# Second attention of a four-layer block: two batches prepared ahead, norms and the copy of K on ScalarE, one Newton chain for two norms

## The reference

```python
x = x + attn_a(layernorm(x), W_attn, b_attn, W_proj, b_proj)   # 16 heads, rotary, causal
x = x + ffn(layernorm(x), expert_sel, keys, values)            # 64 experts, each token to its best 4
x = x + attn_b(layernorm(x), WQ, WK, WV)                       # one head, local band, see below
x = x + ffn(layernorm(x), expert_sel, keys, values)            # the same experts again

def attn_b(inputs, WQ, WK, WV):
    q, k, v = (einsum('bth,hd->btd', inputs, W) for W in (WQ, WK, WV))
    score = einsum('bqd,bkd->bqk', q, k) / sqrt(128)
    score = score * band          # band is 1 within 32 below and 31 above, else 0
    return einsum('bqk,bkd->bqd', softmax(score), v)   # scores outside the band are 0, not -inf

def ffn(x, expert_sel, keys, values):
    sel_val, sel_idx = top_k(sigmoid(xf @ expert_sel.T), 4)
    # sum over the chosen experts of (relu(xf @ keys[e]) * gate) @ values[e]
```

## Time and profile before

| | us |
|---|---|
| median of three runs | 1124.91 |
| lowest and highest | 1121.94, 1127.12 |
| the profiled execution | 1120.72 |
| its span, first to last instruction | 1119.0 |
| mean granted clock of TensorE, as a share of 2.4 GHz | 0.86 |

### The profile page before, as it was taken

How to read it: one execution, slowest core, us unless ns; L and a number is a source line. 1 busy time by engine, 2 the same in 40 slices (tenths; PEclk the granted TensorE clock), 3 DMA queues, 4 the chain that set the end, 5 groups by cost and what they waited for, 6 DMA issues and landing times.

```text
span 1119.0 us, 22668 instructions
## 1 busy us (share of the span) xinstructions
PE 802.9 (72%) x7290; PEld 590.3 (53%) x7290; DVE 752.1 (67%) x2101; ACT 559.8 (50%) x1505; POOL 729.7 (65%) x860
## 2 busy tenths in 40 slices
PE   2799988787878877679789986566478776994000
PEld 0444444444434432669789875445468776993000
DVE  3687898988878842576566788898676773773111
ACT  1167766776747665456546544444436553662000
POOL 6344648898975758665676457777745246666776
PEclk9889999999969988889989996785689898997555
DMA  6455655543237223359868642111156566995222
GB/s 191 135 200 203 210 163 175 189 142 117 67 91 237 61 70 100 107 162 273 240 172 239 180 127 69 48 51 51 49 150 172 147 181 180 263 283 164 71 61 63
DMA packets 206548, 163.82 MB, mean 146 GB/s; under 512 B 15968, under 2 KB 191072, under 8 KB 206432
## 3 DMA queue, kind: packets, MB, share of 16 engines
q1 hardware_dynamic: 183968, 110.43, 34.5%
q0 software_dynamic: 16384, 33.59, 10.4%
q10 hardware_dynamic: 6080, 18.35, 4.4%
HBM read 78.94 MB, written 83.36 MB: 145 GB/s over the span
## 4 chain that ended last, share of the span: by engine, by line
PE 34%; DVE 19%; POOL 19%; issue 12%; DMA 10%; ACT 5%; ACTq 0%; POOLq 0%; DVEq 0%; SPq 0%
PE ps L786 5%; PE ps L687 5%; POOL sorted_rows L1742 4%; PE ps L795 4%; DMA v_aug<-result_rows,dest 3%; PE ps L646 3%; PE ps L775 3%; DMA x_scaled<-result_rows,dest 3%; POOL y_heads L1756 2%; ACT arena L993 2%; POOL arena L1788 2%; POOL x_scaled L1756 2%; DVE row_max L1226 2%; POOL xn L1763 1%; PE ps L734 1%
## 5 line engine op out<-in xcount | busy, mean ns | idle before, releaser
L993 ACT ACTIVATE arena<-ps 128x512 f32<-128x512 f32 x320 | 183.0, 598 | 74.9 <-PE ps L619 73.7
L1742 POOL DMA_INDIRECT sorted_rows<-v_aug,dest x144 | 143.5, 997 | 97.9 <-issue 33.4
L1425 DVE COPY arena<-ps 128x512 f32<-128x512 f32 x128 | 88.1, 689 | 98.7 <-PE ps L775 98.3
L786 PE MATMUL ps<-arena 128*128 128x128 f32 x1024 | 145.6, 288 | 10.4 <-DVE arena L1425 9.1
L646 PE MATMUL ps<-arena 64*128 64x128 bf16 (+3 forms) x576 | 129.9, 305 | 28.8 <-DMA arena<-k_parts 15.2
L1226 DVE TENSOR_REDUCE row_max<-ps 128x1 f32<-128x512 f32 (+1 forms) x192 | 126.8, 681 | 30.6 <-PE ps L666 29.6
L982 ACT COPY arena<-ps 128x512 f32<-128x512 f32 x128 | 74.9, 586 | 144.6 <-PE ps L795 142.3
L786 PEld LDWEIGHTS ps<-arena 128*128 128x128 f32 x1024 | 133.3, 203 | 13.8 <-DVE arena L1425 10.0
L795 PE MATMUL ps<-arena 128*128 x1024 | 138.7, 279 | 0.9 <-ACT arena L982 0.9
L1742 POOL DMA_INDIRECT sorted_rows<-x_scaled,dest x112 | 111.7, 997 | 36.2 <-issue 23.7
L619 PE MATMUL ps<-arena 64*128 64x512 bf16 (+3 forms) x512 | 124.4, 311 | 15.0 <-ACT arena L993 12.4
(11 more groups left out here) (219 smaller groups left out, 1683.4 us busy)
## 6 DMA issues: line engine op xcount, KB each, us to landing
arena<-sorted_rows SPq DMA_DIRECT2D x128, 256.0 KB, 3.9
result_rows<-arena SPq DMA_DIRECT2D x128, 256.0 KB, 2.8
sorted_rows<-arena ACTq DMA_DIRECT2D x16, 1024.0 KB, 5.1
arena<-q_parts SPq DMA_DIRECT2D x16, 512.0 KB, 3.9
arena<-k_parts SPq DMA_DIRECT2D x16, 512.0 KB, 5.0
q_parts<-parts SPq DMA_DIRECT2D x52, 128.0 KB, 2.8
k_parts<-parts SPq DMA_DIRECT2D x38, 128.0 KB, 2.9
sorted_rows<-v_aug,dest POOLq DMA_INDIRECT x144
```

Of the source, the lines that this page charges most:

```text
L786: mm = pe.matmul(ps[:, e_bank(2, layer, half, n), P * i:P * i + P], ktile[:, v, P * i:P * i + P], xtt[:, v, P * i:P * i + P], start=True, ...
L993: nc.scalar.activation(prob[:, grp % 2, pr % 2, PROB_AT[u]:PROB_AT[u] + T], ps[:, v % 2, :], ACT.Exp, scale=SCALE_A).then_inc(exp_done, 1)
L1742: g.indirect_dma_start(sorted_d[b // HALF][:, :], bass.IndirectOffsetOnAxis(dest[:, 16 * b + n:16 * b + n + 1], 0), scaled_rows(layer, b)[ ...
```

## The change

Iteration b now prepares batch b + 2 instead of b + 1, so the loop starts at b = -2 and has one iteration more. The router's norm of batch b is applied in iteration b itself instead of b + 1, so NT and LG move there; choice, ranks, positions, scaling and scatter stay one iteration later. DVE takes the statistics of batch b and of batch b + 2 one after the other and runs one Newton chain on both (`inverse_roots`), which ends in a new small operation, minus mean times inverse root. ACT applies both norms with it as bias and the root as scale (N3 for the router, N2 for the attention: four activations each) and copies K. The four additions of a batch's gathered rows stand at one place of DVE's iteration instead of four. The orders of PE, ACT and DVE, the banks, and the places of the expert steps change with it: (0, 1) has 15, 14 and 5 steps beside iterations -2, -1 and 0; (1, 0) has 8 and 14 beside iterations 7 and 8 and the remaining 12 behind them. POOL's order of transfers and SP's order do not change.

```diff
@@ -87,15 +87,14 @@
 
 
 
-BJOBS = [(1, "S01", 0), (3, "S23", 0), (5, "NT", -1), (6, "LG", -1), (7, "P01", 0), (1, "P23", 0), (3, "XT", 1), (5, "O", 0),
-         (6, "Q", 1), (7, "K", 1), (1, "RK", -1), (3, "V", 1), (5, "VO", 1), (6, "TB", -1)]
-LAST_IT_B = B + 1
+BJOBS = [(1, "S01", 0), (3, "S23", 0), (7, "P01", 0), (1, "P23", 0), (5, "O", 0), (1, "RK", -1), (5, "NT", 0), (3, "XT", 2),
+         (6, "LG", 0), (6, "Q", 2), (7, "K", 2), (3, "V", 2), (5, "VO", 1), (6, "TB", -1)]
+FIRST_IT_B, LAST_IT_B = -2, B + 1
 WIN = 192
 OUTSIDE = T - WIN
 PLACES = 14
-BESIDE = {(0, 1): {-1: (3, 0, 0, 1, 1, 0) + 8 * (1,), 0: PLACES * (1,), 1: 7 * (1, 0)},
-          (1, 0): {6: (0, 0, 0, 0, 0, 0, 1, 1, 1, 1, 1, 1, 1, 0), 7: (1, 0, 1, 1, 0, 1, 1, 1, 1, 0, 1, 0, 1, 0),
-                   8: (1, 1, 1, 1, 1, 1, 0, 1, 0, 1, 1, 1, 0, 1)}}
+BESIDE = {(0, 1): {-2: (3, 1, 1, 0) + 10 * (1,), -1: PLACES * (1,), 0: (1, 0, 1, 0, 1, 0, 1, 0, 1, 0, 0, 0, 0, 0)},
+          (1, 0): {7: 6 * (0,) + 8 * (1,), 8: PLACES * (1,)}}
 
 
...
@@ -896,26 +900,26 @@
                         attention_b(name, b)
 
             apart(0, expert_step)
-            for it in range(-1, LAST_IT_B + 1):
+            for it in range(FIRST_IT_B, LAST_IT_B + 1):
                 attend(it, "S01", "S23")
                 beside(it, 0)
                 beside(it, 1)
+                attend(it, "P01")
+                beside(it, 2)
+                attend(it, "P23")
+                beside(it, 3)
+                attend(it, "O")
+                beside(it, 4)
+                attend(it, "RK")
+                beside(it, 5)
+                beside(it, 6)
                 attend(it, "NT")
-                beside(it, 2)
-                attend(it, "LG", "P01")
-                beside(it, 3)
-                attend(it, "P23")
-                beside(it, 4)
-                attend(it, "O")
-                beside(it, 5)
-                attend(it, "XT")
-                beside(it, 6)
+                beside(it, 7)
+                attend(it, "XT", "LG")
+                beside(it, 8)
...
@@ -1080,7 +1084,22 @@
                 act.wait_ge(bank_ready[bank], n + 1)
                 return ps[:, bank, :], bank_free[bank]
 
+            def apply_norm(i, b, dst, done):
+
+                for t in range(TT):
+                    nc.scalar.activation(dst[:, t, :], x[:, TT * b + t, :], ACT.Identity, bias=negb[:, i, t:t + 1],
+                                         scale=rsb[:, i, t:t + 1]).then_inc(done, 1)
+
             def attention_b(name, b):
+                if name == "N3":
+                    act.wait_ge(shifts, b + 3)
+                    act.wait_ge(scaled, 16 * (B + b - 1))
+                    apply_norm(1, b, xn1[:, b % 2], norm3)
+                    return
+                if name == "N2":
+                    act.wait_ge(shifts, b + 1)
+                    apply_norm(0, b, xn0, norm2)
+                    return
                 if name == "E":
                     act.wait_ge(nrow_done, b + 1)
                     nc.scalar.activation(probw[:, b % 2, :, WIN], nrow[:, b % 2, :], ACT.Exp)
@@ -1099,6 +1118,8 @@
                     nc.scalar.copy(ntt[:, :], o).then_inc(free, 1)
                 elif name == "Q":
                     nc.scalar.copy(qt[b % 2], o).then_inc(free, 1)
+                elif name == "K":
+                    nc.scalar.copy(kt[b % 2], o).then_inc(free, 1)
                 elif name == "V":
                     nc.scalar.copy(va[b % 2], o)
...
@@ -1128,29 +1149,28 @@
 
             apart(0, expert_step)
             act.wait_ge(band_made, BANDS)
-            for it in range(-1, LAST_IT_B + 1):
+            for it in range(FIRST_IT_B, LAST_IT_B + 1):
                 attend(it, "E")
                 beside(it, 0)
                 beside(it, 1)
-                attend(it, "NT")
+                attend(it, "P01")
                 beside(it, 2)
-                attend(it, "LG", "P01")
-                beside(it, 3)
                 attend(it, "P23")
-                beside(it, 4)
-                beside(it, 5)
-                attend(it, "XT")
-                beside(it, 6)
-                attend(it, "Q")
+                for place in (3, 4, 5, 6):
+                    beside(it, place)
+                attend(it, "N3", "N2", "NT")
                 beside(it, 7)
+                attend(it, "XT", "LG")
+                beside(it, 8)
+                attend(it, "Q", "K")
+                beside(it, 9)
                 attend(it, "V")
-                for place in (8, 9, 10):
-                    beside(it, place)
+                beside(it, 10)
...
-                for t in range(TT):
-                    nc.vector.tensor_scalar(dst[:, t, :], src[:, t, :], mv[:, t, 0:1], rs[:, t:t + 1],
-                                            ALU.subtract, ALU.mult).then_inc(seq, 1)
-                    if t % 2:
-                        yield 0.7
-
             roots = count()
 
-            def inverse_root(rs, b, seq, rstd):
-
-                q = 3 * ROOT_STEPS * next(roots)
-                dve.wait_ge(seq, 13 * b + 9)
-                nc.vector.tensor_scalar(guess[:, :].bitcast(I32), rs[:, :].bitcast(I32), -0.5, ROOT_BITS,
-                                        ALU.mult, ALU.add).then_inc(root_seq, 1)
+            def inverse_roots(lo, hi):
+
+                n = next(roots)
+                q = 3 * ROOT_STEPS * n
+                rs, y, half = rsb[:, lo:hi, :], guess[:, lo:hi, :], slope[:, lo:hi, :]
+                nc.vector.tensor_scalar(y.bitcast(I32), rs.bitcast(I32), -0.5, ROOT_BITS, ALU.mult, ALU.add).then_inc(root_seq, 1)
                 for i in range(ROOT_STEPS):
                     dve.wait_ge(root_seq, q + 3 * i + 1)
-                    nc.vector.scalar_tensor_tensor(out=slope[:, :], in0=rs[:, :], scalar=-0.5, in1=guess[:, :],
-                                                   op0=ALU.mult, op1=ALU.mult).then_inc(root_seq, 1)
+                    nc.vector.scalar_tensor_tensor(out=half, in0=rs, scalar=-0.5, in1=y, op0=ALU.mult, op1=ALU.mult).then_inc(root_seq, 1)
                     dve.wait_ge(root_seq, q + 3 * i + 2)
-                    nc.vector.tensor_tensor(slope[:, :], slope[:, :], guess[:, :], ALU.mult).then_inc(root_seq, 1)
+                    nc.vector.tensor_tensor(half, half, y, ALU.mult).then_inc(root_seq, 1)
                     dve.wait_ge(root_seq, q + 3 * i + 3)
                     last = i == ROOT_STEPS - 1
-                    nc.vector.scalar_tensor_tensor(out=(rs if last else guess)[:, :], in0=slope[:, :], scalar=1.5, in1=guess[:, :],
-                                                   op0=ALU.add, op1=ALU.mult).then_inc(rstd if last else root_seq, 1)
+                    nc.vector.scalar_tensor_tensor(out=rs if last else y, in0=half, scalar=1.5, in1=y,
+                                                   op0=ALU.add, op1=ALU.mult).then_inc(rstd_b if last else root_seq, 1)
+                dve.wait_ge(rstd_b, n + 1)
...
@@ -1578,10 +1586,8 @@
                                                          op0=ALU.mult, op1=ALU.add)
                 res.then_inc(free, 1)
                 dve.wait_ge(*evacuated("O", b))
-                if b:
-                    dve.wait_ge(ln3, 13 * b)
-                finish(ln_stats(x[:, TT * b:TT * b + TT, :], st1, mv1, rs1, b, ln3))
-                inverse_root(rs1, b, ln3, rstd3)
+                finish(ln_stats(x[:, TT * b:TT * b + TT, :], st1, mvb[:, 1], rsb[:, 1, :], b, ln3, norm3))
+                dve.wait_ge(ln3, 9 * b + 9)
 
...
@@ -1612,69 +1618,54 @@
 
             apart(0, expert_step)
             dve.wait_ge(band_made, BANDS)
-            for c in range(TOPK):
-                add_rows(0, 0, c)
-
-            for b in range(-1, LAST_IT_B + 1):
-                r, nxt = b - 1, b + 1
-                attend, route, prepare = 0 <= b < B, 0 <= r < B, nxt < B
+
+            for b in range(FIRST_IT_B, LAST_IT_B + 1):
+                r, far = b - 1, b + 2
+                attend, route, prepare = 0 <= b < B, 0 <= r < B, far < B
                 if attend:
                     score_rows(b)
-                beside(b, 0)
-                if route:
-                    dve.wait_ge(scaled, 16 * (B + r - 1))
-                    finish(ln_apply(x[:, TT * r:TT * r + TT, :], mv1, rs1, xn1[:, r % 2], r, ln3, rstd3))
-                beside(b, 1)
-                beside(b, 2)
-                beside(b, 3)
-                if prepare:
-                    combined_stats(nxt)
-                beside(b, 4)
-                if prepare:
-                    if nxt:
-                        bank, n = bjob["XT", b]
-                        dve.wait_ge(bank_ready[bank], n + 1)
-                    finish(ln_apply(x[:, TT * nxt:TT * nxt + TT, :], mv0, rs0, xn0, nxt, ln2, rstd2))
-                add_soon(b + 2, 0)
-                beside(b, 5)
+                for place in (0, 1, 2):
+                    beside(b, place)
                 if route:
```

(65 more changed lines are left out.)

30 lines of the change are left out of this document (10 added, 20 removed).

## The result

| | before | after |
|---|---|---|
| median of four runs, us | 1124.95 | 1148.21 |
| lowest and highest | 1121.94, 1127.12 | 1144.40, 1151.77 |
| the profiled execution, and its span | 1120.72, 1119.0 | 1151.77, 1150.0 |
| granted clock, mean | 0.860 | 0.845 |

After takes 1.0208 times as long, 95% interval 1.0161 to 1.0255. Of the 31.0, 3.7 arise ahead of the second attention: the first product of the experts (0, 1) starts at 557.85 us before and at 561.54 after. That is how executions differ and no cost of the change: in the twelve kernels of the experiments, which are the same as after up to there, it starts between 557.2 and 561.2 us.

A forecast was written before the change was run, and what follows sets the result against it. DVE bounded iterations, POOL second; afterwards ACT's queue would close the loop at 31.7 us. Batch 7's Newton end 870.7 plus 57.5 gave 928.2, gathers 949.0, plus 180.8 and 2.3 a 1132.1 us span; forecast 1138, range 1108 to 1149.

The forecast's parts named there:

- The period: Second attention's loop, one Newton chain end to the next: 31.7 us through ACT's queue, bounds 25.8 and 33.5.
- one hole: DVE's timeline in iterations 2 to 5: idle for 6 us or more ahead of the output product.
- R(1): R(b) is the end of the Newton chain of batch b's router norm; R(1) was forecast at 688.5 us.
- E: ACT's exponentials of the next batch: to start directly behind the sixteenth scaling, without waiting for DVE, 17.4 us into the period.
- The activation: ACT's eight norm activations with scale and bias: 0.30 us each, taken from the scaling's row, upper bound 0.44.
- the first rival: Second attention's loop: DVE still closes it, faster; at a 25.8 us period 1104 us on the median; chance 0.21.
- The 4.6 us that the prediction took off DVE: DVE's work per iteration: norm applications, K's copy and a Newton chain removed, one small operation added; 4.6 of 25.0 us.
- The head: First iterations of the second attention, beside layer 0's expert steps: batch 0's Newton chain ends at 660.6 us, batch 1's 688.5.
- R(7) to the last batch's scatter: From the end of batch 7's Newton chain to the last scatter's start: 57.5 us, against 47.3 before.
- no step ran ahead of R(7): Layer 1, half 0: no expert step ahead of batch 7's Newton chain end; first expert product after 860 us.
- The rest: From the last scatter's start to the end of the span: 201.5 us as before, plus 2.3 for slower gathers.
- the last rival: Slower than forecast: lower clock throughout, activations at 0.40 us, five periods 9 us longer, 1147 us; chance 0.12.

The follow-up runs named there:

- e1: The kernel after, with ACT's sixteen scalings moved from directly ahead of the next iteration's exponentials to later in that iteration: 1130.0 us, ratio to before 1.0063.
- e4: The kernel after, with DVE taking the statistics of batch b+2 ahead of the output of batch b instead of behind it: 1138.5 us, ratio to before 1.0136.
- e6: The kernel after, with 36 and 44 unread identity transposes added in PE's two idle stretches of iterations 1 to 6: 1133.2 us, ratio to before 1.0106.
- e7: The kernel after, its work reordered: next batch's scores, exponentials and transposes issued an iteration earlier, some expert steps moved: 1117.7 us, ratio to before 0.9967.
- e5: The kernel after, with both norms applied by DVE again, directly behind the Newton chain, instead of by ACT: 1141.2 us, ratio to before 1.0158.
- e3: The kernel after, with 11 of the 34 expert steps of layer 1, half 0 placed ahead of batch 7's Newton chain end: 1152.4 us, ratio to before 1.0235.

## Why the prediction was right, step by step

**The period, right, with one hole misplaced.** Predicted 31.7, measured 32.4, 31.8, 32.6 and 31.8 us from R(1) to R(5). In iteration 3, from R(2): LG's activation done at 6.5 (5.9 predicted), Q's product at 8.6 (8.1), K's at 10.1 (9.8), VO's copy at 12.7 (12.6), scalings at 17.5 (17.4), output at 25.1 (25.4). E starts directly behind the scalings, and the clock is 0.50 at NT and in the product and 1.00 at V, as said; e1, e4 and e6 each moved the term that they were meant to. But V had the upper level only in the two periods of 31.8 us, where it took 1.05 and 1.10; in those of 32.4 and 32.6 it took 1.69 and 1.91, at a clock of 0.59 and 0.50, which is about what the periods differ by. PE's V from R(2) and from R(3):

```profile
736.74 1.05 PE L853 MATMUL ps<-w_b,xnt 128*128 128x128 f32 x8
768.73 1.91 PE L853 MATMUL ps<-w_b,xnt 128*128 128x128 f32 x8
```

What the sum missed is that PE's scores stand behind VO: DVE, which was to reach its maxima about 10 us behind R, waits there 4.2 us. So its idle time came in two holes, 4.2 and 3.9, not one of 6, and the scalings' 4.8 us were worth only 3.

**The activation, mis-sized.** Eight norm activations took 3.19 us, 0.40 each, against the 0.30 taken from the scaling's row; the bound was 0.44. In iteration 3 the 0.7 us are gone by V's product, which ended at 11.0, where it was predicted, since K's, 1.67 us, ran partly at the upper level; from R(1) and R(3) it ended at 11.8 and 12.0. The Trainium skill, "ScalarE: Activation LUTs", section "What ACT_TABLE_LOAD costs", gives 186 ns and 0.833 ns for each element, 93 ns for each pointer operand, and an overlap of 93 between neighbours. An estimate from that is 386 ns for the scaling and 479 for the norm; the trace has means of 386 and 479 in this iteration. The second pointer is what made the scaling the wrong neighbour. Groups of ACT in iteration 3 of after (busy us, mean ns, idle before):

```profile
L963 ACT ACTIVATE v_aug<-xn,gates 128x128 f32<-128x128 f32 x16 | 4.8, 386 | 0.0
L1090 ACT ACTIVATE xn<-x_res,neg_mean_rs_b,rs_b 128x128 f32<-128x128 f32 x8 | 3.2, 479 | 10.5 <-DVE neg_mean_rs_b L1221 10.5
```

**DVE as the bound, the first rival: refuted in this order.** The Trainium skill's rule to optimise the busiest engine first ("Perfetto Trace Analysis", section "Identifying the Most-Contended Engine") would have given it. The trace agrees with the rule only in e7, where the order lets DVE close the loop: it is busy for 21.8 us of 24.5 and never waits longer than 0.74. Here the change took work off the busiest engine and the kernel became 2% longer, and putting 2.2 us an iteration back (e5) cost nothing. The 4.6 us that the prediction took off DVE were too many as well: its busy time in the iteration fell by 3.1 (25.0 to 21.9).

**The head, 6.3 us late:** R(0) at 666.9 instead of 660.6. 3.7 us is the later start named above, 2.6 the sum's own. From R(1) to R(7), 185.1 us instead of 182.2.

**R(7) to the last batch's scatter, mis-sized: 63.2 us instead of 57.5, outside the bounds of 53 to 61.** The destinations took 60.3. That is the 47.0 us that they took before and six steps at 2.22, so the 3.1 us that the sum took off, mostly for work removed from DVE, did not show; no run tested this. A further 3.0 is a releaser that changed: before, that scatter waited for DVE; now for ACT's first scaling, which stands behind a copy of an expert's result. I had taken the destinations for the scatter. That no step ran ahead of R(7) held but for the first one's transposes, 0.64 us on PE at 876.96 us, 2.5 ahead of it (before, the first are at 813.28); e3 shows that placing more ahead would have won nothing.

**The rest, 207.3 us instead of 203.9:** the gathers were to run 2.3 us longer than before and ran 3.6 longer, and the last batch's sixteen scatters took 22.8 us instead of 20.7. What slowed these transfers was not tried.

These terms, 6.3 and 2.5 for R(7), 5.7 and 3.4, make the trace's 1150.0 us out of 1132.1. On the medians the forecast of 1138 is 10 us short, and 1148.2 lies only 0.8 below the upper end of its range: the period and its reasons were right, the size of the whole was narrowly inside. The time is nearer to the last rival's 1147, but not for that rival's reasons. Its activations at 0.40 us came, its lower clock throughout did not; its 9 us were to come from five periods, and R(1) to R(7) is only 2.9 longer than predicted. The rest came from the head and the tail.

## What to carry to other kernels

With in-order queues, ask what the next pass of a loop stands behind on each engine: the price of a move is what it puts ahead of that, and the busiest engine need not be on it. When work is moved off one engine, place it behind the instruction that the others wait for; here moving sixteen scalings won 16 us, and each part of the work taken off DVE, put back alone, cost none that the runs can tell. Looking a batch further ahead costs an iteration at the start, 28.8 us here between R(1) of the two traces, 3.7 of them the later start, before it can win anything. Then look for the queue that is second, here POOL's, before you count a gain twice.

## What the hardware showed that I had not expected

An activation of 128x128 with two pointer operands follows its neighbour at 0.39 us, one with a single pointer at 0.29. Four transposes of 128x128 take 0.63 us at clock 1.00 and 1.09 at 0.50; in a row of 36 at 1.00 one takes 0.11 (4.10 us). The clock in e6 was kept up by work that nobody reads: in the iteration where it stood at 1.00 PE's longest wait was 1.2 us, and Q took 1.12 instead of 2.07 us; behind R(2), where XT took 1.09 us again, PE had waited 1.9 us ahead of NT.
